# Sixteen expert tiles of a decoder layer run between the last eleven steps of its attention part

## The chip, the core and the metric

One core of one Trainium2 chip runs the whole kernel. The metric is the device time of one execution in microseconds (us), lower is better. The engines are TensorE (PE in the profile; PEld is its weight load), VectorE (DVE), ScalarE (ACT), GpSimd (POOL) and SyncE (SP). Each runs its own queue of instructions strictly in order and waits for the others through semaphores; SyncE and GpSimd also issue the DMAs.

## The reference, cut to what matters

```python
def reference(x, ctx, mask, ...):                       # x: (4, 1024, 256)
    # linear attention, 16 heads of 16
    q, k, v = softmax(x @ Wq.T + bq), softmax_over_tokens(x @ Wk.T + bk), x @ Wv.T + bv
    a = layernorm(q @ (k.T @ v)) * ln_g + ln_b
    x = layernorm(x + a @ Wo.T + bo)
    # cross attention, 8 heads of 32 over 77 context rows, masked
    x = layernorm(x + softmax(x/sqrt(32) @ K.T + b + mask) @ V)
    # mixture of experts: 8 experts, the best 4 of each token
    w, idx = top_k(softmax(x @ router_w), 4);  w = w / w.sum()
    y = sum_j w_j * gelu(x @ up_w[idx_j]) @ down_w[idx_j]     # 256 -> 1024 -> 256
    return layernorm(x + y)
```

The layer norms of the last two lines have neither scale nor shift. All inputs and outputs are float32.

## The kernel before

4096 tokens in four batches are 32 token tiles of 128. The kernel has two parts, one after the other.

**Attention (`attention`).** A software pipeline of 49 steps (`STEPS`) over the token tiles. Each step does one stage for each of up to six tiles: `a` the projections to queries, keys and values, and `c0` to `c4` (`chain_tile(s, d)`) the later stages of older tiles: head outputs and first normalization (`c0`, `out`, tile `Z`), output projection, residual and second normalization (`c1`, `wo`, `X1`), logits against the context (`c2`, `lg`), probabilities turned and multiplied by the context values (`c3`, `pa`, `pb`, `pv`, result `X2`), and the third normalization, the turned tile and the router's logits (`c4`, `x2`, `rt`). Every ninth step has no tile and closes a batch (`closing`). From step 35 on there are no new tiles (`a`), so steps 38 to 48 only drain `c0` to `c4`; step 38 has no `c3`, step 39 no `c4`, step 44 no `c0`, step 45 no `c1`, and so on. The third normalization needs GpSimd twice: `second_residual` adds `X1` to `X2` (line 532), and `inverse_deviation` makes the reciprocal deviation (lines 519 and 521), in the next step. In every step GpSimd does its work in a fixed order: deviations, two record scatters, second residual, residual bias (line 527), two record scatters.

For each half batch VectorE ranks the experts (`choose`, `gates`), and GpSimd scatters one 64-byte record (token, weight) per token and expert into `slot_records` in DRAM (line 548, 128 DMAs in all). `store_tile` writes each finished tile to `token_sums` (float32) and `token_rows` (split in two float16 parts). Beside this the expert weights come in as 16 pieces of 1 MB (`PIECE_STEPS`, the last at step 40) and are split into float16 pairs by ScalarE and VectorE (lines 616 and 707).

After the last step VectorE makes the tile tables (`tile_tables`, lines 843 to 886): which expert a tile belongs to, where its records lie, and three scales.

**Experts (`experts`).** 72 tiles, 63 of 256 slots and 9 of 128. For each, SyncE loads the records (line 1240), GpSimd gathers the token rows (`gather`, line 1273), SyncE turns them with DMA transposes (line 1247), TensorE makes the up products (line 1321, 48 matmuls in four groups, each in one of four PSUM banks), ScalarE the gelu (line 1359), VectorE splits the result into two halves (lines 1396 and 1398), TensorE makes the down products (line 1335, 48 matmuls), ScalarE scales by the gate (line 1367) and GpSimd adds the result to `token_sums` by an indirect DMA (`result`, line 1282). TensorE does the up products of tile t before the down products of tile t - 1. At the end the sums are loaded, normalized and stored. All memory of the attention part is free for the experts, since the parts do not overlap.

## Time and profile before

| | us |
|---|---|
| median of 3 runs (lowest to highest) | 1327.94 (1326.01 to 1328.0) |
| the profiled execution | 1324.53 |
| its span, first to last instruction | 1322.5 |
| TensorE busy | 1124.3 (85%) |
| VectorE busy | 744.9 (56%) |
| GpSimd busy | 660.8 (50%) |
| ScalarE busy | 477.0 (36%) |

The span falls into three parts. Up to 523 us the attention steps run, with all engines in use and none of them full. From 523 to 559 us TensorE does next to nothing: the last records, the tables and the first gather. From 559 to 1280 us the experts run with TensorE always busy. The last 42 us are the final normalization. Times in the rows are microseconds from the start of the span.

### The profile page before, as it was taken

How to read it: one execution, taken by the hardware profiler on the slowest of the kernel's cores; microseconds unless marked ns; L12 is line 12 of the kernel's file. 1: busy time of each engine (PE TensorE's matmuls, PEld its weight loads, DVE VectorE, ACT ScalarE, POOL GpSimd, SP SyncE). 2: the span in 40 equal slices, each digit the busy share in tenths (PEclk: the TensorE clock that was granted, in tenths of full speed). 3: DMA queues.
4: the chain of work that ended last, by engine and by line, in shares of the span. 5: the costliest groups of instructions: out<-in, count | busy, mean ns of one | idle time of the engine just before them, and what ended most of it. 6: DMA issues, size and time to landing. Idle time of an engine off the chain costs nothing.

```text
span 1322.5 us, 26761 instructions
## 1 busy us (share of the span) xinstructions
PE 1124.3 (85%) x8570; PEld 924.5 (70%) x8570; DVE 744.9 (56%) x1803; ACT 477.0 (36%) x896; POOL 660.8 (50%) x769
## 2 busy tenths in 40 slices
PE   5569888888987872099999999999999999999980
PEld 3246665655665652088888888888888888888860
DVE  2667868777887774264444555444555444454325
ACT  3754434434533430033333333333333333333223
POOL 3023437737757776534445555445555444554424
PEclk9779879878977875599999999999999999999995
DMA  6531212222221110145444444444444445443426
GB/s 199 161 109 46 75 34 78 80 64 58 67 69 48 57 36 24 40 65 81 76 79 78 79 78 79 79 78 80 75 78 80 81 75 79 79 78 61 66 38 254
DMA packets 159965, 103.78 MB, mean 78 GB/s; under 512 B 104908, under 2 KB 151168, under 8 KB 159584
## 3 DMA queue, kind: packets, MB, share of 16 engines
q1 hardware_dynamic: 129824, 65.62, 19.4%
q0 software_dynamic: 30016, 36.46, 17.1%
q8 instruction: 83, 1.36, 0.4%
q14 instruction: 42, 0.34, 0.1%
HBM read 50.38 MB, written 33.95 MB: 64 GB/s over the span
## 4 chain that ended last, share of the span: by engine, by line
PE 55%; DMA 1%; DVE 1%; POOL 1%; issue 1%; SPq 0%; ACT 0%; ACTq 0%; POOLq 0%; DVEq 0%
PE psu L1321 28%; PE psy L1335 27%; POOL frstd L1298 1%; DMA token_sums<-y,rec 1%; DVE fstat L1419 1%; DMA sums<-token_sums 0%; DVE sums L1411 0%; DMA xT<-xg 0%; SPq L1239 0%; POOL fvar L1296 0%; SPq L1240 0%; DVE fmv L1422 0%; SPq L1247 0%; ACT sums L1378 0%; ACTq L1156 0%
## 5 line engine op out<-in xcount | busy, mean ns | idle before, releaser
L1321 PE MATMUL psu<-xT,w_up 128*128 128x256 f16 (+1 forms) x3456 | 379.8, 268 | 37.3 <-DMA xT<-xg 37.3
L1282 POOL DMA_INDIRECT token_sums<-y,rec x135 | 223.8, 1658 | 332.5 <-ACT y L1367 308.1
L1321 PEld LDWEIGHTS psu<-xT,w_up 128*128 x3456 | 326.5, 98 | 80.7 <-issue 38.8
L1335 PE MATMUL psy<-w_down,hh 128*128 x2160 | 357.6, 273 | 0.0
L1335 PE MATMUL psy<-w_down,hl 128*128 x1080 | 294.4, 273 | 0.0
L1359 ACT ACTIVATE h<-psu,up_scale 128x512 f32<-128x512 f32 x270 | 185.5, 687 | 179.8 <-PE psu L1321 135.7
L1335 PEld LDWEIGHTS psy<-w_down,hh 128*128 128x128 f16 x2160 | 211.2, 98 | 25.6
L1398 DVE SCALAR_TENSOR_TENSOR hl<-h,h_scale,hh 128x512 f16<-128x512 f32 x270 | 202.9, 752 | 9.6
L1396 DVE TENSOR_SCALAR hh<-h,h_scale 128x512 f16<-128x512 f32 x270 | 132.3, 490 | 91.1 <-ACT h L1359 78.9
L1386 DVE TENSOR_SCALAR gate<-rec,y_scale 128x2 f32<-128x2 f32 (+1 forms) x72 | 16.3, 227 | 292.9 <-ACT y L1367 279.5
L1367 ACT ACTIVATE y<-psy,gate 128x256 f32<-128x256 f32 x135 | 57.1, 470 | 312.0 <-PE psy L1335 312.0
L1273 POOL DMA_INDIRECT xg<-token_rows,rec x135 | 133.7, 990 | 52.6 <-issue 40.2
L548 POOL DMA_INDIRECT slot_records<-recs,posi x128 | 131.2, 1025 | 40.2 <-issue 31.7
L1335 PEld LDWEIGHTS psy<-w_down,hl 128*128 128x128 f16 x1080 | 105.6, 98 | 12.1
L519 POOL TENSOR_SCALAR ve<-mv 128x1 f32<-128x1 f32 x96 | 24.1, 251 | 169.3 <-DVE mv L715 167.5
L1053 PE MATMUL big<-wqkv,xinT 128*128 128x512 f32 x128 | 73.5, 704 | 4.0 <-ACT xinT L597 4.0
L521 POOL TENSOR_TENSOR rstd<-ve,nhalf 128x1 f32<-128x1 f32 x96 | 57.0, 594 | 8.1 <-POOL ve L519 0.2
L1120 PE MATMUL small<-vx,pT 128*128 128x99 f32 (+2 forms) x320 | 48.3, 304 | 9.0 <-ACT pT L604 9.0
L1120 PEld LDWEIGHTS small<-vx,pT 128*128 128x128 f32 (+1 forms) x320 | 43.5, 213 | 15.2 <-ACT pT L604 12.0
L1110 PE MATMUL big<-kbd,x1T 128*128 128x308 f32 x128 | 51.2, 484 | 0.0
L999 PE MATMUL trans<-ident,X 128*128 128x128 f32 x128 | 29.3, 315 | 23.9 <-DVE X L719 19.6
L532 POOL TENSOR_TENSOR X<-X 128x256 f32<-128x256 f32 x32 | 32.5, 1014 | 32.1 <-DVE L L969 17.9
(213 smaller groups left out, 1286.9 us busy)
## 6 DMA issues: line engine op xcount, KB each, us to landing
w_down<-in_L_ffn_up_w_dram SPq DMA_DIRECT2D x8, 1024.0 KB, 5.2
w_down<-in_L_ffn_down_w_dram SPq DMA_DIRECT2D x7, 1024.0 KB, 5.8
XA<-in_x_dram SPq DMA_DIRECT2D x32, 128.0 KB
XRES<-in_x_dram SPq DMA_DIRECT2D x32, 128.0 KB
token_sums<-X SPq DMA_DIRECT2D x32, 128.0 KB
token_rows<-XR SPq DMA_DIRECT2D x32, 128.0 KB, 1.7
sums<-token_sums SPq DMA_DIRECT2D x8, 512.0 KB, 6.6
out_dram<-sums SPq DMA_DIRECT2D x8, 512.0 KB, 2.6
```

Of the source, the lines that this page charges most:

```text
L521: pool.tensor_tensor(rstd[:, kind, at:at + 1], ve[:, kind, at:at + 1], nhalf[:, 0:1], ALU.pow).then_inc(rstd_ready[kind], 1)
L548: pool.indirect_dma_start(slots, bass.IndirectOffsetOnAxis(ap=posi[:, half, e:e + 1], axis=0), recs[:, half, e // TOPK, e % TOPK, :], None ...
L1053: pe.matmul(dst[:, 0:2 * C], xT[:, c, :], wqkv[:, c, C:3 * C], start=(c == 0), stop=(c == CC - 1))
L1120: ins = pe.matmul(dst[:, h0 * (XD + 1):h1 * (XD + 1)], pT[0:n, c, :], vx[0:n, c, 0:h1 - h0, :].rearrange("p h d -> p (h d)"), start=(c == ...
L1273: pool.indirect_dma_start(xg[:, t % 2, j, :], None, rows, bass.IndirectOffsetOnAxis(ap=rec[:, t % RING, j, 0:1], axis=0)).then_inc(xg_load ...
L1282: pool.indirect_dma_start(acc, bass.IndirectOffsetOnAxis(ap=rec[:, t % RING, j, 0:1], axis=0), y[:, t % 2, j, :], None, compute_op=ALU.add ...
L1321: ins = pe.matmul(psu[use % UBANKS][:, i * size(t):(i + 1) * size(t)], w[:, ws, c, m:m + P], xT[:, t % 2, xs * CC + c, 0:size(t)], start=( ...
L1335: ins = pe.matmul(ytile(t)[:, j, :], (hh, hl)[hs][:, t % 2, c, j * P:(j + 1) * P], w[:, ws, c, :], start=(n == 0), stop=(n == 3 * HC - 1))
L1359: act.activation(h[:, use % UBANKS, :], psu[use % UBANKS][:, :], ACT.Gelu_apprx_tanh, scale=k["up_scale"][:, t:t + 1]).then_inc(gelu_ready, 1)
L1367: act.activation(y[:, t % 2, j, :], ytile(t)[:, j, :], ACT.Copy, scale=gate[:, t % 2, j:j + 1]).then_inc(y_ready, 1)
L1396: dve.tensor_scalar(hi, hf, k["h_scale"][:, t:t + 1], None, ALU.mult).then_inc(hh_ready, 1)
L1398: dve.scalar_tensor_tensor(out=lo, in0=hf, scalar=k["h_scale"][:, t:t + 1], in1=hi, op0=ALU.mult, op1=ALU.subtract).then_inc(hl_ready, 1)
```

## The change

The first sixteen of the 63 full expert tiles are made from the tokens of batches 0 and 1 alone, whose records are complete by step 35. Every expert's whole tiles of 256 slots are taken from them (`taken`), so that the number of tiles stays 72.

- **One part.** `attention` and `experts` become one function `layer`. `Q` and `K` are separate tensors; the experts' buffers lie over `K`, `wqkv`, `xinT`, `XA` and `V`, which are free from step 38 on.
- **Early copies.** The tiles of batches 0 and 1 are stored to `early_sums` instead of `token_sums`, and to `early_rows` as well as `token_rows`. At the end of step 35 SyncE copies their records to `early_records` (8 DMAs of 128 KB); scatters of batch 2 wait for it (`records_copied`). The last weight piece comes at step 36 instead of 40 and waits for the last key sums.
- **Early tables.** VectorE makes the sixteen early slots in step 36 (`early_slots`) and experts and scales in step 37 (`factors`, `early_scales`). At the end of step 37 GpSimd gathers tiles 0 and 1.
- **Mixed steps.** Steps 38 to 48 (`MIX0` on) each have one expert tile, cut in four groups. TensorE's up products of group i and down products of group i - 2 (`LAG`) stand between the stages of the attention. All up products of these steps go to one PSUM bank, all down products to another. ScalarE copies the turned tiles first and then does the group's gelu; `exp_logits` moves to the next step. GpSimd gathers tile t + 2 after the first two deviations, and adds the result of tile t - 1 at the end of the step.
- **Behind them.** Tiles 11 to 15 run beside the last sixteen scatters (eight before each of two results) and the late tables, which VectorE does in four pieces behind four groups' halves. After tile 15 the records come from `slot_records`; between tiles 18 and 19 SyncE copies `early_sums` to `token_sums` (16 DMAs of 128 KB), and the result of tile 16 waits for it.
- **Groups throughout.** All 72 tiles run as groups with a lag of two, with 3 PSUM banks for up products instead of 4, 2 gelu buffers instead of 4 and 4 buffers for halves.

```diff
-PIECE_STEPS = [2, 3, 4, 5, 6, 7, 8, 9, 12, 16, 20, 24, 28, 32, 36, 40]
+PIECE_STEPS = [2, 3, 4, 5, 6, 7, 8, 9, 12, 15, 18, 21, 24, 28, 32, 36]
+EARLY = 16
+MIX0 = PIECE_STEPS[-1] + 2
+LAG = 2
+HALF_RING = 4
+H_RING = 2
...
+def up_bank(i):
+    return 0 if i < MIXED_GROUPS else (i - MIXED_GROUPS) % 3
...
+                if s == record_step(EARLY_BATCHES) - 1:
+                    for half in range(HALVES):
+                        sp.wait_ge(scattered[half], 16 * HT * TOPK * EARLY_BATCHES)
+                    for e in range(EXP):
+                        at = slice(e * CAP, e * CAP + EARLY_BATCHES * N)
+                        sp.dma_start(slots1[at, :], slots[at, :]).then_inc(records_copied, 16)
+                if s == MIX0 - 2:
+                    for t in range(4):
+                        records(t)
+                if s >= MIX0 - 1:
+                    turned_rows(s - MIX0 + 1)
...
             def scatter(b, half, at, n):
                 pool.wait_ge(records_ready, HALVES * b + half + 1)
+                if b == EARLY_BATCHES:
+                    pool.wait_ge(records_copied, 16 * EXP)
...
+                if s >= MIX0:
+                    gather(s - MIX0 + 2)
...
+                if s == MIX0 - 1:
+                    gather(0)
+                    gather(1)
+                if s > MIX0:
+                    result(s - MIX0 - 1)
+            for t in range(MIXED, ETILES):
+                if t + 2 < ETILES:
+                    gather(t + 2)
+                if t < MIXED + 2:
+                    scatter(B - 1, HALVES - 1, (t - MIXED) * HT * TOPK // 2, HT * TOPK // 2)
+                result(t - 1)
+            result(ETILES - 1)
...
+            for i in range(MIXED_GROUPS - 1, NGROUPS):
+                t, g = GROUP[i]
+                halves(i)
+                if i == MIXED_GROUPS:
+                    late_blocks()
+                if i == MIXED_GROUPS + 1:
+                    late_experts()
+                if i == MIXED_GROUPS + 2:
+                    late_slots()
+                if i == MIXED_GROUPS + 3:
+                    late_scales()
...
+            for i in range(MIXED_GROUPS, NGROUPS):
+                up_products(i)
+                down_products(i - LAG)
```

TensorE in a mixed step of the changed kernel, in the code's own words (each call is one group or one stage):

```python
up_products(i);  turn("z", c1);  turn("q", c0);  down_products(i - LAG)
turn_second(c4);  turn("x1", c2);  heads_out(c0);  up_products(i + 1)
route(c4);  project(c1);  down_products(i + 1 - LAG);  turn_shares(c3)
up_products(i + 2);  context_logits(c2);  down_products(i + 2 - LAG)
context_values(c3);  up_products(i + 3);  down_products(i + 3 - LAG);  positions(s)
```

VectorE's order in such a step is: moments of `c4`, halves of group i - 1, normalization of `c4`, halves of i, head outputs of `c0` with their sums, row gates, router logits, first sum of `c1`, halves of i + 1, normalizations of `c0` and `c1`, low rows of `c4`, halves of i + 2, logits of `c2`, shares and values of `c3`, routing, sums of `c3`.

How the queues read at the places that the prediction speaks of. GpSimd, one full step before (step 42), from the deviation of `c4` to the last scatter; `X<-X` is the second residual and `XRES<-XRES,cvec` the residual bias:

```order
L519 TENSOR_SCALAR ve<-mv 128x1 [waits mv_ready2]
L521 TENSOR_TENSOR rstd<-ve,nhalf 128x1 [waits ve_ready2]
L519 TENSOR_SCALAR ve<-mv 128x1 [waits mv_ready0]
L521 TENSOR_TENSOR rstd<-ve,nhalf 128x1 [waits ve_ready0]
L519 TENSOR_SCALAR ve<-mv 128x1 [waits mv_ready1]
L521 TENSOR_TENSOR rstd<-ve,nhalf 128x1 [waits ve_ready1]
L548 DMA slot_records<-recs,posi 32768x16 [waits records_ready]
L548 DMA slot_records<-recs,posi 32768x16
L532 TENSOR_TENSOR X<-X 128x256 [waits sm_free,x1_ready]
L527 TENSOR_TENSOR XRES<-XRES,cvec 128x256 [waits xres_loaded0]
L548 DMA slot_records<-recs,posi 32768x16 [waits records_ready]
L548 DMA slot_records<-recs,posi 32768x16
```

GpSimd, the same stretch of the changed kernel, from the second residual of one step to the gather of the next:

```order
L766 TENSOR_TENSOR X<-X 128x256 [waits sm_free,x1_ready]
L761 TENSOR_TENSOR XRES<-XRES,cvec 128x256 [waits xres_loaded0]
L784 DMA slot_records<-recs,posi 32768x16 [waits records_copied,records_ready]
L784 DMA slot_records<-recs,posi 32768x16
L814 DMA early_sums<-y,rec 2048x256 [waits y_added0,y_ready]
L814 DMA early_sums<-y,rec 2048x256
L753 TENSOR_SCALAR ve<-mv 128x1 [waits mv_ready2]
L755 TENSOR_TENSOR rstd<-ve,nhalf 128x1 [waits ve_ready2]
L753 TENSOR_SCALAR ve<-mv 128x1 [waits mv_ready0]
L755 TENSOR_TENSOR rstd<-ve,nhalf 128x1 [waits ve_ready0]
L798 DMA xg<-early_rows,rec 128x256 [waits rec_loaded7,xt_loaded1]
L798 DMA xg<-early_rows,rec 128x256
```

Two result DMAs now stand between a step's scatters and the next step's deviation of `c4`, and two gathers between the deviations of `c0` and `c1`. ScalarE before, in a full step (`pr<-pr` is the exponential of the logits):

```order
L597 ACTIVATE zT<-trans 128x256 [waits tr_ready]
L597 ACTIVATE qT<-trans 128x256 [waits tr_ready]
L597 ACTIVATE x1T<-trans 128x256 [waits tr_ready]
L604 ACTIVATE pT<-trans 128x512 [waits sm_ready,tr_ready]
L604 ACTIVATE pT<-trans 104x128 [waits sm_ready,tr_ready]
L664 ACTIVATE XR<-X 128x256 [waits rows_stored1,x2_ready]
L597 ACTIVATE x2T<-trans 128x256 [waits tr_ready]
L668 ACTIVATE pr<-pr 128x616 [waits big_free]
```

ScalarE in a full mixed step of the changed kernel, up to its second gelu and the results behind it (`h<-big` is a gelu):

```order
L876 ACTIVATE zT<-trans 128x256 [waits tr_ready]
L876 ACTIVATE qT<-trans 128x256 [waits tr_ready]
L919 ACT_TABLE_LOAD
L919 ACTIVATE pr<-pr 128x616 [waits big_free]
L876 ACTIVATE x2T<-trans 128x256 [waits tr_ready]
L876 ACTIVATE x1T<-trans 128x256 [waits tr_ready]
L907 ACT_TABLE_LOAD [waits hl_ready]
L907 ACTIVATE h<-big,up_scale 128x512 [waits up_ready]
L925 ACTIVATE XR<-X 128x256 [waits rows_stored0,x2_ready]
L907 ACTIVATE h<-big,up_scale 128x512 [waits hl_ready,up_ready]
L883 ACTIVATE pT<-trans 128x512 [waits sm_ready,tr_ready]
L883 ACTIVATE pT<-trans 104x128 [waits sm_ready,tr_ready]
```

The first gelu now stands behind the copies of both turned tiles and a table load, and a second load stands before the exponential. TensorE in the changed kernel, at the turn of the second sum (`X`, from `X2` and then `X1`) in a full step:

```order
L1683 MATMUL big<-w_down,hh 128x256 x2
L1683 MATMUL big<-w_down,hl 128x256
L1534 MATMUL trans<-ident,X 128x128 [waits tr_copied,x2_ready]
L1534 MATMUL trans<-ident,X 128x128
L1534 MATMUL trans<-ident,X 128x128 [waits tr_copied,x1_ready]
L1534 MATMUL trans<-ident,X 128x128
L1575 MATMUL small<-state,qT 128x136 [waits sm_free,tr_copied]
L1575 MATMUL small<-state,qT 128x136
L1664 ISA [waits gelu_ready]
L1664 MATMUL big<-xgT,w_up 128x256 x2
```

Before, the turn of the second sum ended a step's products and the router product followed it; now the second up group of the tile stands behind it and waits for the first group's gelu.

## Rows read from the trace of the kernel before

**Rows 1.** Windows: stretch, its length, busy (count) by engine, granted clock, DMA share, GB/s
```profile
core 0: us, PE busy (x) PEld busy (x) DVE busy (x) ACT busy (x) POOL busy (x), PEclk, DMA share, GB/s
415.30:523.20 107.90, 71.05 (x328) 53.06 (x328) 68.88 (x218) 29.46 (x68) 77.24 (x108) 0.71 0.16 46
523.20:559.00 35.80, 0.02 (x1) 0.03 (x2) 13.11 (x37) 1.49 (x2) 20.40 (x20) 0.50 0.13 28
```

**Rows 2.** The chain that ended last, start of the expert part: start, length, what
```profile
554.92 1.31 SPq L1247
...
558.98 13.48 PE psu L1321 x96
572.46 5.24 PE psy L1335 x48
```

**Rows 3.** Timeline of TensorE, steps 37 to 40: start, length, instruction, idle before
```profile
414.24 0.42 PE L999 MATMUL trans<-ident,Z 128*128 128x128 f32 x2
...
419.73 0.30 PE L1111 MATMUL big<-mbf,one 1*128 1x308 bf16 x1
423.37 0.69 PE L999 MATMUL trans<-ident,X 128*128 128x128 f32 x2 [3.34 <-DVE X L719]
...
437.11 0.41 PE L999 MATMUL trans<-ident,X 128*128 128x128 f32 x2 [1.58 <-ACT zT L597]
...
443.80 0.38 PE L999 MATMUL trans<-ident,QK 128*128 128x128 f32 x2
```

**Rows 4.** Instructions grouped by line and shape: count, busy us, mean ns, idle before
```profile
L1398 DVE SCALAR_TENSOR_TENSOR hl<-h,h_scale,hh 128x512 f16<-128x512 f32 x270 | 202.9, 752 | 9.6
L1359 ACT ACTIVATE h<-psu,up_scale 128x512 f32<-128x512 f32 x270 | 185.5, 687 | 179.8 <-PE psu L1321 135.7 <-DVE hl L1398 28.3 <-issue 15.6
...
L1396 DVE TENSOR_SCALAR hh<-h,h_scale 128x512 f16<-128x512 f32 x270 | 132.3, 490 | 91.1 <-ACT h L1359 78.9 <-issue 7.7
...
L950 DVE SCALAR_TENSOR_TENSOR pr<-big,bcol,xmb 128x616 f32<-128x616 f32 x32 | 27.2, 851 | 0.1
...
L938 DVE TENSOR_REDUCE xm<-big 128x8 f32<-128x616 f32 x32 | 25.5, 796 | 9.0 <-PE big L1111 8.7
...
L1352 ACT ACT_TABLE_LOAD x1 | 1.3, 1283 | 29.1 <-PEq L208 29.1
```

**Rows 5.** Timeline of GpSimd, step 37's end and step 38's first deviation
```profile
418.12 0.73 POOL L532 TENSOR_TENSOR X<-X 128x256 f32<-128x256 f32 x1
418.80 0.73 POOL L527 TENSOR_TENSOR XRES<-XRES,cvec 128x256 f32<-128x256 f32 x1
...
420.98 0.96 POOL L548 DMA_INDIRECT slot_records<-recs,posi  x1 [0.30 <-issue]
421.97 0.24 POOL L519 TENSOR_SCALAR ve<-mv 128x1 f32<-128x1 f32 x1
422.30 0.57 POOL L521 TENSOR_TENSOR rstd<-ve,nhalf 128x1 f32<-128x1 f32 x1
```

**Rows 6.** Timelines of GpSimd (first gather, a result) and ScalarE (a tile's results)
```profile
550.84 0.99 POOL L1273 DMA_INDIRECT xg<-token_rows,rec  x1 [6.11 <-DMA rec<-slot_records]
...
641.81 1.62 POOL L1282 DMA_INDIRECT token_sums<-y,rec  x1 [4.26 <-ACT y L1367]
643.74 1.70 POOL L1282 DMA_INDIRECT token_sums<-y,rec  x1 [0.30 <-issue]
...
640.70 0.84 ACT L1367 ACTIVATE y<-psy,gate 128x256 f32<-128x256 f32 x2 [4.63 <-PE psy L1335]
```

**Rows 7.** Instructions grouped by line: the split of a weight piece on VectorE
```profile
L707 DVE SCALAR_TENSOR_TENSOR w_down<-V,wsc,w_down 128x2048 f16<-128x2048 f32 x1 | 2.3, 2335 | 0.0
```

**Rows 8.** DMA issues: count, KB each, median us from issue to landing
```profile
w_down<-in_L_ffn_up_w_dram SPq DMA_DIRECT2D x8, 1024.0 KB, 5.2
```

**Rows 9.** Timeline of VectorE: the first and the last instruction of the tables
```profile
523.06 0.17 DVE L843 TENSOR_SCALAR QK<-QK 128x32 f32<-128x32 f32 x1
...
536.36 0.75 DVE L886 TENSOR_REDUCE y_scale<-QK 128x72 f32<-128x576 f32 x1
```

## What I predict, and why

> **What bounds the kernel now.** I read the windows first, then the timelines around two places, then the groups of instructions by line. The windows [rows 1] show three stretches. From 559 us on, TensorE is busy without a gap at full clock, and the rows of the chain [rows 2] give 5.24 us for each half of a tile: an expert tile is worth 10.48 us of TensorE, and nothing but TensorE work bounds it. Before it lie 35.8 us in which TensorE does nothing (last records, tables, first gather). Before that, attention steps 38 to 48 take 107.9 us with TensorE busy for 71.1 us, at a mean granted clock of 0.71. So the change aims at a real hole: 263.0 us pass from the first TensorE instruction of step 38 (414.24, [rows 3]) to the end of the eleventh tile's work (558.98 + 11 x 10.48 + 3.0 for the slow first 96 products of [rows 2] = 677.3). A full step's attention products fit in 6.7 us at full clock (437.11 to the next step's turn of the queries at 443.80, [rows 3]), and I count 50 us for the eleven. With 115.3 us of tiles that is 165 us, 98 us below what is spent now. The question is how much of the 98 the order of the queues gives back.
>
> **A mixed step, from gelu to gelu.** I follow the loop through the engines from G, the end of the step's first gelu; TensorE may then start the second up group, since all groups of the mixed steps share one bank. One group is 1.31 us up and 1.31 us down (a quarter of 5.24).
> TensorE: up 1.3, router products 0.5; the projection waits until VectorE has done two halves (0.49 + 0.75, [rows 4]) and the head sums, so it starts near 2.1 and ends at 3.0; down 4.3, turned shares 5.0, third up group 6.3. ScalarE has by then to copy the shares and send two results (2 x 0.42, [rows 6]), so the third gelu (0.69) ends at 7.6. VectorE does its halves until 9.0, then maximum 0.80, shift 0.23, subtraction 0.85, reciprocal and values some 0.6 [rows 4]: about 11.6 with the small gaps.
> GpSimd: the second residual waits for these values. It takes 0.73 and behind it stand, in this order, the residual bias (0.73), two scatters (2 x 1.27, [rows 5]), and the two result DMAs of the tile before (2 x 1.66 + 2 x 0.30 = 3.9, [rows 6]), and only then the deviation for the next step (0.24 + 0.57, [rows 5]): 20.7. This is the step that I find decisive. The result DMAs, 3.9 us, are issued in front of the deviation on which everything that follows waits.
> Then VectorE scales the tile (0.41, 21.2), TensorE turns it (0.4, as the turn at 443.80 in [rows 3]) and ScalarE copies it (0.9 with the gaps), the copy of the other turned tile adds 0.3, a table load 1.28 [rows 4], the gelu 0.69: the next G is at **24.5 us**. TensorE's work in that time is 17.1 us; it idles 5 us before the turn and 2.5 us before the second up group.
>
> Without scatters and bias (step 44) the same walk gives 20.6; with eight scatters but fewer chains, steps 45 and 46 give 24.5 and 21.5. Step 47 has no exponentials of logits but the shares in step 48 force two table loads between gelus; with four groups each for 47 and 48, the last one ends 20.0 later. Step 38 has no down products, results or second residual, and its end is set by ScalarE (two copies, load 1.28, exponential 0.72, copy, load 1.28, gelu), which gives 17.0 from its G to that of step 39.
>
> ScalarE's switches themselves: [rows 4] shows 1.28 us for a load with the next activation right behind it (the warming gelu that opens the expert part), after a long idle time. The Trainium skill, "ScalarE: Activation LUTs", section "What ACT_TABLE_LOAD costs", says that a switch also drains the engine for about 1.38 us, 2.66 us in all. The row shows the load alone, and no row has a load right behind other work, so the trace neither confirms nor excludes the drain; by the page the ten gelu loads would add some 14 us (an estimate from its figure), by the row nothing.
>
> **Before the first gelu.** (a) All 16 weight pieces are now done before step 38, one more than now: 2.33 us of VectorE and five small instructions [rows 7] on an engine with little room, 2.5 us. (b) In step 36 GpSimd's scatters wait for the copy of the records, which SyncE issues after the last weight piece (at 396.3, when the sums of keys are done): 1 MB in 5 to 6 us each (w_down lands in 5.2, [rows 8]), so near 407 instead of 402.3, 4.7 us. The sixteen small instructions for the early slots (about 0.3 us apiece: 31 take 14.0 us in [rows 9]) run on VectorE in the same time and are hidden by it; alone they would cost the same. (c) The first gather stands behind step 37's last scatter, which ends at 421.94 [rows 5]. Before, the first gather starts at 550.84, the transposes at 554.92 and the product at 558.98 [rows 6, 2], 8.1 us from end to end; with 0.3 of gap that is 430.4, and TensorE, whose queue has the up group ahead of step 38's turns, stands from 414.24: 16.2 us. (d) Up group, turns, copies, load and gelu on an engine at half clock (2.6 + 1.8 + 3.1): 7.5 us.
> Sum until G of step 38: 30.9 us.
>
> **After the mixed steps.** Two down groups are left over, 2.6 us. VectorE then has the late tables: 14.0 us in before (523.06 to 537.1, [rows 9]), and about as much with more but smaller instructions, cut into four pieces behind the halves of four groups. Four groups last 10.5 us on TensorE; halves (5.0) and tables (14.0) take VectorE 19.0. Of the 8.5 us too much the lag of two groups covers 0.9, since the halves before come late too: **7.6 us** of stall on TensorE. The sixteen last scatters (2 x 10.2 us on GpSimd) delay the gathers of tiles 14 and 15 to within a microsecond of need; the copies of 2 MB of sums hold one result for about 8 us where the next gather has 20. Both I cost at nothing, and name them as a rival.
>
> **Clock.** Where TensorE has waited 3.3 us (419.96 to 423.37, [rows 3]) its next turn takes 0.69 us where two such products take 0.38 at full clock; in the empty stretch before the experts the granted clock is 0.50 [rows 1], the 1.2 GHz level, and at 558.98 the slow start behind it cost 3.0 us [rows 2]. With a 7.5 us hole in every mixed step I expect this in ten of them. At most 3.0 us each, at least nothing; some of the slow time lies beside VectorE and GpSimd, so I take half, 15 us.
>
> **The sum.** 30.9 + 17.0 + 5 x 24.5 (steps 39 to 43) + 20.6 + 24.5 + 21.5 + 20.0 + 2.6 = 259.6 us, plus 15 for the clock: 274.6 against 263.0, 11.6 longer, and 7.6 for the tables: 19.2 us. The other 56 tiles' worth and the final norms stay: the groups are cut finer, but per group of 2.62 us VectorE needs 1.24 and ScalarE 0.69. The profiled execution took 1324.5 us (span 1322.5); with 19.2 it is 1343.7. The median of the runs is 3.4 us above it, so I forecast **1347 us**, 1330 to 1362 for this case (loop within 1 us a step, clock between 8 and 25).
>
> **Rivals.**
> *First, faster.* The results do not sit on the loop: GpSimd's order costs nothing because the values come early enough. Then the limit is TensorE's own 17.1 us plus the wait for z, q, exponential, two copies, two loads and gelu (about 3.5 us), 20.5 per step. Five steps win 4.0 each, steps 45 and 46 win 6.5 together: 26 us; the holes shrink to 3 us and the 15 us of clock go: 1347 - 41 = 1306. It decides if the second residual starts before about 8 us after G rather than at 11.7. For it: GpSimd is busy only some 17 of 24.5 us, and reported times overlap by a tenth each, so serial addition is too dear. Against: the order rows show no instruction that could move. 25%, with all between 1306 and 1325.
> *Second, more scarcity behind the mixed steps.* Scatters, the 2 MB of copies and gathers on one GpSimd queue starve tiles 14 to 20: each scatter burst is 10.2 us where GpSimd has 4 us of room per tile (10.48 less 3.9 for results and 2.6 for gathers), so up to 2 x 6 = 12 us: 1359. 10%.
> *Third, still slower.* The table switches cost double when the engine was working (at most another 1.28 on ten gelu loads, 13 us, as an engine in work may show what the idle one of [rows 4] does not; the mechanism is the one of the page named above) and the slow clock takes its full 3.0 in each step (15 more): 1347 + 28 = 1375. For it: no hole of 3 us in before leaves the clock high. 17%.
> *Fourth,* steps and tiles do not mix and simply add: 107.9 + 115.3 = 223.2 us, 39.8 less than 263.0, of which the start takes 30.9 and the tables 7.6, so 1.3 us are won: 1327. It is the case in which the change does not do what it says; it lies inside the range, 6%.
>
> **Chances.** Forecast and its surroundings above 1331: 42%; first rival 25%; second 10%; third 17%; fourth rival 6%. A measurement of this kernel can tell about 0.2% from no change, here 1325.3 to 1330.6. Faster 0.27 (the first rival and a little of the last), same 0.05, slower 0.68. The range leaves out the extreme halves of the first and third rival: 1308 to 1372.
>
> **What would show it.** Right: GpSimd's result rows directly before the deviation row in steps 40 to 43, VectorE idle on the deviation for several us, steps of 24 to 27 us, a hole on TensorE before the turn of the second sum, granted clock below 0.9 between 440 and 700; first up product near 438; tile 11 near 686. Wrong: steps of 20 us with TensorE released by gelu only, clock above 0.95; or holes on TensorE between tiles 14 and 20; or more than 1.3 us between a ScalarE copy and the gelu behind a load. Wrong too if the first up product comes before 430.

## The result, and the profile after

| | before | after |
|---|---|---|
| median (lowest to highest), us | 1326.97 (1325.80 to 1328.00), 4 runs | **1365.95** (1363.79 to 1367.62), 4 runs |
| after / before | | 1.0294, 95% interval 1.0281 to 1.0307 |
| the profiled execution, its span | 1324.53, 1322.5 | 1363.79, 1361.9 |
| TensorE busy, mean granted clock | 1124.3, 0.906 | 1136.4, 0.898 |

The kernel became 39 us slower. The prediction said slower, 1347 us, in a range of 1308 to 1372: direction and range held, but the sum of +19 us was only half of what came, and the narrower range given for the forecast's own case, 1330 to 1362, did not hold. The windows of the changed kernel answer to [rows 1]:

```profile
core 0: us, PE busy (x) PEld busy (x) DVE busy (x) ACT busy (x) POOL busy (x), PEclk, DMA share, GB/s
436.90:686.00 249.10, 187.87 (x1318) 151.47 (x1319) 116.49 (x290) 85.76 (x147) 125.76 (x136) 0.83 0.26 48
...
692.00:726.00 34.00, 21.53 (x147) 15.04 (x145) 19.62 (x54) 4.62 (x8) 22.19 (x21) 0.78 0.24 40
...
780.00:900.00 120.00, 119.88 (x1099) 107.19 (x1097) 58.56 (x103) 40.33 (x68) 63.91 (x47) 1.00 0.54 92
```

From 780 us on all is as it was: TensorE all but full (119.88 of 120 us), 10.48 us a tile. The time is lost in three places:

| place | before | after | lost | forecast |
|---|---|---|---|---|
| from 414.24 to the first product of the twelfth tile | 674.7 (677.3 less the 2.6 that still belong to the eleventh) | 690.8 | 16.1 | 11.6 |
| from there to the last product | 608.0 | 627.8 | 19.8 | 7.6 |
| behind the last product | 39.5 | 43.0 | 3.5 | 0 |

The first row gives points in time, the others lengths. The last products of TensorE start at 1282.72 before and at 1318.62 after, 35.9 us apart; 19.8 is what is left when 16.1 is taken off.

**Inside a mixed step.** The loop that the prediction called decisive stands in the trace as described. Timelines of GpSimd, VectorE, TensorE and ScalarE from the end of step 40 into step 41 (start, length, instruction, in brackets the idle time before it and what ended it):

```profile
500.74 0.42 DVE L1353 TENSOR_TENSOR X<-small,xr 128x256 f32<-128x256 f32 x1
501.31 0.72 POOL L766 TENSOR_TENSOR X<-X 128x256 f32<-128x256 f32 x1 [2.75 <-DVE X L1353]
...
502.53 0.18 DVE L1057 BATCH_NORM_AGGREGATE mv<-stat 128x2 f32<-128x6 f32 x1
502.87 1.09 POOL L784 DMA_INDIRECT slot_records<-recs,posi  x1
504.27 0.96 POOL L784 DMA_INDIRECT slot_records<-recs,posi  x1 [0.30 <-issue]
505.53 1.63 POOL L814 DMA_INDIRECT early_sums<-y,rec  x1 [0.30 <-issue]
507.46 1.58 POOL L814 DMA_INDIRECT early_sums<-y,rec  x1 [0.30 <-issue]
508.49 0.85 POOL L753 TENSOR_SCALAR ve<-mv 128x1 f32<-128x1 f32 x1
509.43 0.57 POOL L755 TENSOR_TENSOR rstd<-ve,nhalf 128x1 f32<-128x1 f32 x1
510.03 0.41 DVE L1061 TENSOR_SCALAR X<-X,mv,rstd 128x256 f32<-128x256 f32 x1 [6.14 <-POOL rstd L755]
510.50 1.12 PE L1534 MATMUL trans<-ident,X 128*128 128x128 f32 x4 [4.37 <-DVE X L1061]
511.65 0.38 ACT L876 ACTIVATE x1T<-trans 128x256 f32<-128x256 f32 x1
512.06 1.28 ACT L907 ACT_TABLE_LOAD   x1
513.35 0.69 ACT L907 ACTIVATE h<-big,up_scale 128x512 f32<-128x512 f32 x1
514.18 2.74 PE L1664 MATMUL big<-xgT,w_up 128*128 128x256 f16 x12 [1.65 <-ACT h L907]
```

The moments are ready at 502.7; the deviation (L753) that needs them starts at 508.49, behind two scatters and two result transfers. VectorE waits 6.14 us for it and TensorE 4.37 us for VectorE. The up group behind the hole takes 2.74 us instead of 1.48, the length that the same row has at full clock.

**Behind the mixed steps** stands something that the prediction did not have. TensorE and GpSimd of the changed kernel beside tile 11:

```profile
692.95 0.99 POOL L784 DMA_INDIRECT slot_records<-recs,posi  x1 [0.30 <-issue]
...
701.86 0.95 POOL L784 DMA_INDIRECT slot_records<-recs,posi  x1 [0.30 <-issue]
...
697.50 0.38 PE L1664 MATMUL big<-xgT,w_up 128*128 128x256 f16 x2 [0.94 <-issue]
698.94 0.27 PE L1664 MATMUL big<-xgT,w_up 128*128 128x256 f16 x1 [1.06 <-issue]
700.35 0.38 PE L1664 MATMUL big<-xgT,w_up 128*128 128x256 f16 x2 [1.14 <-issue]
701.80 0.59 PE L1664 MATMUL big<-xgT,w_up 128*128 128x256 f16 x2 [1.06 <-issue]
703.91 0.58 PE L1664 MATMUL big<-xgT,w_up 128*128 128x256 f16 x2 [1.52 <-issue]
```

An up group and a down group together usually take TensorE 2.6 us. Here one or two products come every 1.4 us, and the profile knows no engine or transfer that they wait for ("issue"). This goes on while GpSimd issues its eight scatters, one every 1.27 us, and again from 717 to 726 us beside the next eight. Between 697.5 and 706.2 the DMA engines are busy for 2% of the time, so it is not their traffic. VectorE works on meanwhile, one small instruction every 0.2 us from 697.15 to 698.79. What TensorE waits for between 690 and 780 us, in sum (us, times, longest):

```profile
PE big L1664 <- issue: 9.0, 10, 1.5
PE big L1683 <- ACT y L915: 1.8, 1, 1.8
PE big L1683 <- issue: 1.7, 2, 1.0
```

### The profile page after: what moved, and what is told of

It reads as the page before. It is cut to its first block, busy times and chain, and to the rows that moved or that the text cites. A ratio compares the mean times of both kernels' runs of the same rounds, so it can differ in the third digit from the quotient of the medians.

```text
span 1361.9 us, 27063 instructions
## 1 busy us (share of the span) xinstructions
PE 1136.4 (83%) x8572; PEld 926.6 (68%) x8572; DVE 752.8 (55%) x1831; ACT 496.6 (36%) x913; POOL 673.0 (49%) x768
## 4 chain that ended last, share of the span: by engine, by line
PE 65%; DVE 10%; POOL 10%; issue 5%; ACT 4%; DMA 4%; SPq 1%; ACTq 0%; POOLq 0%; DVEq 0%
PE big L1664 26%; PE big L1683 13%; PE trans L1683 11%; POOL slot_records L784 3%; PE big L1706 2%; PE big L1605 2%; POOL rstd L755 2%; PE small L1584 2%; PE trans L1534 2%; POOL early_sums L814 2%; PE small L1752 2%; PE small L1616 1%; ACT L907 1%; PE small L1629 1%; POOL X L766 1%
## 5 line engine op out<-in xcount | busy, mean ns | idle before, releaser
L1664 PE MATMUL big<-xgT,w_up 128*128 128x256 f16 (+1 forms) x3456 | 422.8, 272 | 48.6 <-ACT h L907 21.1
L1664 PEld LDWEIGHTS big<-xgT,w_up 128*128 x3456 | 329.3, 100 | 101.8 <-issue 57.8
L907 ACT ACTIVATE h<-big,up_scale 128x512 f32<-128x512 f32 x270 | 185.5, 687 | 459.1 <-PE big L1664 439.1
L1683 PE MATMUL big<-w_down,hh 128*128 x1264 | 221.0, 277 | 3.7 <-ACT y L915 2.0
L1683 PE MATMUL big<-w_down,hl 128*128 x632 | 174.7, 276 | 0.0
L1683 PE MATMUL trans<-w_down,hh 128*128 x896 | 153.9, 274 | 0.0
L1683 PEld LDWEIGHTS big<-w_down,hh 128*128 128x128 f16 x1264 | 125.0, 100 | 21.8 <-issue 4.2
L753 POOL TENSOR_SCALAR ve<-mv 128x1 f32<-128x1 f32 x96 | 29.0, 303 | 217.3 <-DVE mv L1057 216.0
L1683 PE MATMUL trans<-w_down,hl 128*128 x448 | 122.6, 274 | 0.0
L1683 PEld LDWEIGHTS trans<-w_down,hh 128*128 128x128 f16 x896 | 87.9, 98 | 11.1
L814 POOL DMA_INDIRECT early_sums<-y,rec x32 | 53.1, 1661 | 35.9 <-ACT y L915 28.4
L1683 PEld LDWEIGHTS big<-w_down,hl 128*128 128x128 f16 x632 | 62.7, 99 | 9.4 <-issue 1.6
```

Source lines behind the costliest of these rows:

```text
L814: pool.indirect_dma_start(acc1 if t < EARLY else acc, bass.IndirectOffsetOnAxis(ap=rec[:, t % RING, j, 0:1], axis=0), y[:, t % 2, j, :], N ...
L907: act.activation(h[:, i % H_RING, :], psu[up_bank(i)], ACT.Gelu_apprx_tanh, scale=k["up_scale"][:, t:t + 1]).then_inc(gelu_ready, 1)
L1664: ins = pe.matmul(psu[up_bank(i)][:, j * size(t):(j + 1) * size(t)], w[:, ws, c, m:m + P], xgT[:, t % 2, xs * CC + c, 0:size(t)], start=(n ...
L1683: ins = pe.matmul(ytile(t)[:, j, :], (hh, hl)[hs][:, i % HALF_RING, at:at + P], w[:, ws, c, :], start=(c == 0 and j == 0 and hs == 0 and w ...
```

## The experiments

All are the changed kernel with one or two edits. The kernel before was run beside each; its medians were 1325.4, 1326.8, 1327.1 and 1326.3 us in the four sittings, so differences of medians across sittings are good to about 2 us. "Gain" is against 1365.95.

| kernel | median (lowest to highest) | / before, 95% interval | gain |
|---|---|---|---|
| e1 results behind the deviation | 1337.66 (1336.96 to 1339.42) | 1.0090 (1.0065 to 1.0115) | 28.3 |
| e2 without the last 16 scatters | 1350.33 (1347.41 to 1351.58) | 1.0177 (1.0149 to 1.0205) | 15.6 |
| e3 these scatters in fours | 1355.78 (1349.62 to 1361.53) | 1.0218 (1.0171 to 1.0265) | 10.2 |
| e4 one mixed step | 1318.90 (1317.90 to 1320.85) | 0.9949 (0.9933 to 0.9964) | 47.1 |
| e5 = e1 and e3 | 1329.94 (1329.43 to 1338.99) | 1.0033 (1.0017 to 1.0050) | 36.0 |
| e6 no table switches | 1348.45 (1346.13 to 1350.01) | 1.0160 (1.0141 to 1.0179) | 17.5 |
| e7 = e4, scatters in twos | 1308.02 (1306.38 to 1309.66) | 0.9850 (0.9832 to 0.9869) | 57.9 |
| e8 = e7 with two mixed steps | 1308.47 (1307.83 to 1308.92) | 0.9853 (0.9837 to 0.9869) | 57.5 |
| e9 = e7, early gathers | **1305.64** (1302.67 to 1308.77) | 0.9839 (0.9825 to 0.9852) | 60.3 |
| e10 24 filling products a step | 1358.97 (1358.71 to 1364.89) | 1.0243 (1.0227 to 1.0259) | 7.0 |
| e11 = e1, e2 and e6 | 1302.22 (1299.23 to 1305.54) | 0.9817 (0.9798 to 0.9836) | 63.7 |
| e12 40 filling products a step | 1361.63 (1358.14 to 1362.47) | 1.0263 (1.0247 to 1.0280) | 4.3 |

### e1: the results behind the next deviation

```diff
                 if c4 is not None:
                     inverse_deviation(2, c4)
+                if s > MIX0 + 1:
+                    result(s - MIX0 - 2)
...
-                if s > MIX0:
-                    result(s - MIX0 - 1)
+            if MIXED >= 2:
+                result(MIXED - 2)
             for t in range(MIXED, ETILES):
```

> On GpSimd the adding transfers of an early tile (result, 3.9 us in two instructions) stand behind the next step's second deviation (inverse_deviation(2, c4)) instead of before it; nothing else changes. Theory of the loop: in the step from 498.3 to 514.2 us VectorE's moments are there early and the deviation starts only at 508.49, behind two transfers that end at 509, so each of the ten steps gives back 2.5 to 3.9 us, and the slower clock a part more: 1366 comes down to 1328 to 1341. Rival one (the transfers only move: the deviation of the first norm and the gather now stand behind them): 5 to 12 us gained, 1354 to 1361. Rival two (the step is set by VectorE's and TensorE's own order, GpSimd has slack): within 3 us of 1366.

28.3 us: the theory of the loop. The same place in e1, GpSimd and TensorE:

```profile
502.62 0.96 POOL L784 DMA_INDIRECT slot_records<-recs,posi  x1 [0.30 <-issue]
503.60 0.25 POOL L753 TENSOR_SCALAR ve<-mv 128x1 f32<-128x1 f32 x1
503.94 0.57 POOL L755 TENSOR_TENSOR rstd<-ve,nhalf 128x1 f32<-128x1 f32 x1
504.70 1.80 POOL L814 DMA_INDIRECT early_sums<-y,rec  x1 [0.19 <-issue]
...
505.01 0.66 PE L1536 MATMUL trans<-ident,X 128*128 128x128 f32 x4 [0.52 <-DVE X L1063]
508.45 1.48 PE L1666 MATMUL big<-xgT,w_up 128*128 128x256 f16 x12 [2.31 <-ACT h L909]
```

The deviation now stands behind the scatters alone. TensorE waits 0.52 us instead of 4.37, and both the turn and the up group run at full clock. From the first gelu of step 38 to that of step 47 it is 198.6 us instead of 224.1. The gain is the loop's and, with it, what the shorter hole gives back in clock (0.910 for 0.898 over the span). So an order of two lines on an engine that is half idle was worth 28 us, and the kernel that moves them is still 12 us slower than the one before.

### e2 and e3: the last sixteen scatters

e2 takes the two bursts of eight away (and lowers to fit what SyncE waits for ahead of tile 16), so it leaves out those tokens' records; e3 keeps them, four beside each of four tiles, ahead of the gather of that turn:

```diff
+                if t < MIXED + SPREAD:                      # e3: SPREAD = 4; e2: these lines are left out
+                    scatter(B - 1, HALVES - 1, (t - MIXED) * HT * TOPK // SPREAD, HT * TOPK // SPREAD)
                 if t + 2 < ETILES:
                     gather(t + 2)
-                if t < MIXED + 2:
-                    scatter(B - 1, HALVES - 1, (t - MIXED) * HT * TOPK // 2, HT * TOPK // 2)
```

> The last sixteen record scatters (the second half of the last batch), which stand in two bursts of eight beside tiles 11 and 12, are left out, so those tokens' records are missing and part of the output is not the reference's; the tables on VectorE stay. Theory of the scatters (TensorE gets its products about 1.4 us apart just while GpSimd issues a scatter every 1.27 us): TensorE works through 697 to 726 us without the pauses, and 19.6 us lost behind tile 11 come down to 5 to 9: 1366 falls to 1352 to 1356. Rival (the late tables on VectorE hold back the halves and so everything): 0 to 3 us gained, 1363 to 1366.

> The same sixteen scatters, four beside each of tiles 11 to 14 instead of eight beside tiles 11 and 12, put before the gather of the same turn. Theory of the scatters, price by the piece (each holds TensorE up by its 1.27 us whatever stands around it, about 0.8 us lost): nothing changes, 1363 to 1369. Theory of the burst (only a long row of them drains what TensorE has ready): 5 to 10 us gained, 1356 to 1361. Rival (the tables alone cost the time): within 3 us, and TensorE's pauses stay at 697 to 726 us while the scatters are elsewhere.

The same 34 us in e2 and e3 (columns as above; 21.53 us of TensorE work and clock 0.78 in the changed kernel):

```profile
692.00:726.00 34.00, 29.02 (x247) 24.41 (x245) 25.81 (x68) 8.46 (x14) 12.87 (x11) 0.95 0.38 67
...
692.00:726.00 34.00, 27.98 (x195) 19.84 (x194) 22.81 (x57) 7.20 (x13) 20.00 (x18) 0.80 0.29 47
```

Without the scatters 247 products are recorded instead of 147, and no wait of the kind "issue" is left in that stretch. What it does wait for there is the tables' doing:

```profile
PE big L1681 <- DVE hl L1302: 2.5, 3, 1.5
PE trans L1681 <- DVE hl L1302: 2.5, 1, 2.5
```

Those 5.0 us are a wait for VectorE, behind the late tables. The gain of e2 is not all TensorE's. In the profiled executions its first product of the twelfth tile comes 2.1 us later (692.91 for 690.80, a difference that is there before the first scatter is left out), from there to the last product it takes 615.8 us instead of 627.8, 12.1 less, and from the start of that last product to the end of the span 39.7 instead of 43.3, 3.6 less. So the scatters keep TensorE waiting for about 12 us, and of the 19.8 us lost in this stretch 7.7 remain for the tables, where 7.6 had been forecast.

e3 gains 10 of e2's 15.6 us with all scatters still there. Its four runs lie 12 us apart (by its interval the gain is 5 to 18 us), but all lie below the 1363 to 1369 that a price by the piece would give. So the price isn't one by the piece: it hangs on how long GpSimd issues transfers without a break. (e3 and e7 also put the scatters ahead of the gather; no run has the one change without the other.) In e3 GpSimd's transfers (scatters, gathers, results) follow each other unbroken from 692.5 to 711.5 us, and the pauses of TensorE lie between 698 and 713; beside its next row, eight transfers from 720.2 us on, there are two short ones, and beside six transfers from 734.5 to 743.1 us none.

### e4: one mixed step instead of eleven

```diff
-MIX0 = PIECE_STEPS[-1] + 2          # 38
+MIX0 = 48
...
+TABLES0 = PIECE_STEPS[-1]
...
-                if s == MIX0 - 2:                   # early_slots(); early_scales() one step later
+                if s == TABLES0:
```

> MIX0 is 48 instead of 38, with the early tables still built in steps 36 and 37: ten steps run as plain attention steps, one early tile runs in step 48, and 15 run behind the attention beside the last records and tables. Theory (mixing costs more than it hides; the gain of the early tables is only the hole of 35.8 us at the end of the attention): ten plain steps at about 10.2 us each and ten tiles at 10.5 us against 249 us for the mixed stretch save 40 to 50 us: 1316 to 1326, faster than the kernel before by 2 to 12 us. Rival one (the first gather, which waits for records and rows, leaves the same start hole of 16 us at step 48): 1330 to 1340. Rival two (the mixed steps are as good as separate ones and the loss is elsewhere): 1355 to 1366.

47.1 us, and faster than the kernel before by 6. Ten attention steps without tiles and ten tiles without attention are quicker than the ten mixed: from 414 to 530 us the steps run as plain attention steps, then come tiles of 10.48 us. The late scatters and tables together cost what they did: from the first gelu of the second tile to that of the third (545.79 to 575.57) it is 29.8 us where 10.48 are due, 19.3 too many, with the same pauses (7.0 us of "issue") beside one row of 20 transfers.

### e5: e1 and e3 together

> e1_result_later and e3_scatters_in_fours together, eleven mixed steps as in the changed kernel. Theory (two separate losses, 28 us in the mixed steps and about 10 behind them): they add up, 1326 to 1331, level with the kernel before. Rival (with the early tiles done sooner the same wait returns at the late records or sums): 1334 to 1338.

1329.94 us: they add up nearly (28.3 + 10.2 = 38.5, measured 36.0). Two of the ten runs took 1338 and 1339 us; the profile is of one of them, so I read no places from it.

### e6: no table switches

```diff
-                act.activation(h[:, i % H_RING, :], psu[up_bank(i)], ACT.Gelu_apprx_tanh, scale=...
+                act.activation(h[:, i % H_RING, :], psu[up_bank(i)], ACT.Gelu_apprx_tanh if i >= MIXED_GROUPS else ACT.Copy, scale=...
```

> The gelus of the eleven mixed steps' groups are plain copies of the same shape with the same scale, so ScalarE loads no table between them and the exponentials; the values of the early tiles are wrong. Everything else as in the changed kernel. The prediction counted 1.28 us on the path for the gelu table of each step: with one load on the path in ten steps 13 us go, 1350 to 1356. Rival one (a switch also drains the engine, 2.66 us in all): 27 us or more, 1334 to 1341. Rival two (both loads of a step are on the path): about 24 us, 1338 to 1344. Rival three (the load hides in ScalarE's wait): 0 to 4 us.

17.5 us, between the theory's 13 and rival one's 27; the copies leave the early tiles' values wrong. From step 38's first gelu to step 47's it is 208.3 us instead of 224.1, 1.76 per step. The table of instructions by line shows what went, in the changed kernel:

```profile
L907 ACT ACT_TABLE_LOAD x10 | 12.8, 1283 | 0.2
L919 ACT ACT_TABLE_LOAD x8 | 10.3, 1283 | 0.1
```

If the ten loads before the gelus, 12.8 us, are all on the path, as the timeline above has it, the eight before the exponentials (10.3 us) cost the other 3 to 5. The timeline above shows the load at 512.06, 0.03 us behind the end of the copy at 511.65 + 0.38, and the gelu 0.01 us behind the load. The Trainium skill, "ScalarE: Activation LUTs", section "What ACT_TABLE_LOAD costs", adds a drain of about 1.38 us to the load. No row here has room for it, and 1.76 us per step for two switches is well under its 2.66 for one.

### e7 to e9: towards a kernel that gains

e7 takes e4 and e3's lines with `SPREAD = 8`; e8 has `MIX0 = 47` and e1's order besides; e9 is e7 with

```diff
-                if s == MIX0 - 2:
+                if s == TABLES0 + 2:               # SyncE: records(0) to records(3) in step 38
...
+                if s == TABLES0 + 4:
+                    turned_rows(0)
...
-                if s == MIX0 - 1:
+                if s == TABLES0 + 4:               # GpSimd: in step 40
                     gather(0)
                     gather(1)
```

> e4_one_mixed_step with its sixteen last scatters two at a time beside tiles 1 to 8, before the gather of the same turn. In e4 the tiles behind the first lose about 19 us while GpSimd issues eighteen transfers in 28 us without a break. Theory of the burst (TensorE runs out of products only behind some 6 us of unbroken transfers on GpSimd): two scatters, two gathers and two results take 9 of 10.5 us with a break in between, so 12 to 16 us are gained: 1303 to 1307. Rival (a price by the piece, or the tables on VectorE): 1315 to 1320.

> As e7, but with MIX0 at 47: steps 47 and 48, which hold only the last pieces of the attention, each take a tile, with the adding transfers behind the second deviation. In the changed kernel step 47 with its tile takes 14.0 us and 48 11.6, while a tile alone takes 10.5 and a plain step about 10. Theory (a step without the first norms has room for a tile): 2 to 6 us below e7. Rival (the records for the last batch then come later and the late tables wait for VectorE): as e7 or up to 5 us above it.

> As e7_one_mixed_in_twos, but the records of the first four early tiles are loaded in step 38 and the rows of tiles 0 and 1 gathered and turned in step 40, eight steps before they are used; in e7 TensorE waits 7.15 us for the turned rows of tile 0 at 530.2 and then runs at half clock. Theory: this wait goes, and some of the slow clock behind it: 4 to 10 us below e7, 1298 to 1304. Rival (the last attention step, whose turn waits 9.65 us for VectorE, takes the time instead): 1306 to 1310.

e7 is 10.9 us below e4, a little less than the 12 to 16 I had expected. With two scatters a tile TensorE's waits of the kind "issue" sum to 0.5 us. The 34 us behind the attention in e4, and in e7:

```profile
549.00:583.00 34.00, 21.88 (x136) 14.78 (x134) 18.86 (x49) 5.81 (x10) 21.07 (x20) 0.75 0.17 29
...
549.00:583.00 34.00, 28.98 (x259) 24.70 (x258) 25.19 (x61) 9.65 (x17) 20.92 (x18) 1.00 0.37 62
```

GpSimd is busy for the same 21 us in both, with 20 and 18 instructions, and only TensorE's count differs, 136 against 259. This is the cleanest pair: the same sixteen scatters begin at the same place and are spaced otherwise, and the time behind the last product is the same in both. e8 is e7 over again (1308.47): a second mixed step neither gains nor loses. e9 is 2.4 us better than e7, less than the 4 to 10 expected. TensorE's wait for the turned rows (7.15 us in e7) is gone, and the up group follows the last attention step at once, at 528.06. But that step's turn of the second sum comes 5.0 us later (the first line is e7's, the second e9's):

```profile
520.85 0.69 PE L1537 MATMUL trans<-ident,X 128*128 128x128 f32 x2 [9.65 <-DVE X L1064]
...
525.81 0.69 PE L1540 MATMUL trans<-ident,X 128*128 128x128 f32 x2 [9.64 <-DVE X L1067]
```

Most of the 5 us are lost in one place. GpSimd's second residual starts 0.7 us later than in e7 in step 40 (455.87 for 455.15) and 5.0 us later in step 41 (470.21 for 465.18). In between e9 issues its four gathers, from 460.00 to 464.77 us, in front of the deviation for the next step, which starts at 464.80; in e7 it starts at 459.00, right behind the scatters. It is e1's lesson once more: transfers ahead of the small instruction on which the next stage waits. The up groups of this tile run at half clock in both (2.74 us, three times).

The intervals of e7 and e9 touch (the two were run in different sittings, which alone can move a difference by about 2 us), so e9's own gain is likely rather than shown. Against the kernel before it is 21.4 us, 1.6%.

### e10 and e12: what the clock costs

```diff
                 if i >= LAG:
                     down_products(i - LAG)
+                if i >= LAG and c4 is not None:
+                    idle = turn_into(("x2", c4))[:, :, :].rearrange("p a b -> p (a b)")[:, CC * P:CC * P + FILL_COLUMNS]   # 192
+                    for _ in range(FILL):           # 24 in e10, 40 in e12
+                        pe.matmul(idle, k["wu"][:, 0, 0, 0, 0:P], k["wu"][:, 0, 0, 0, 0:FILL_COLUMNS], start=True, stop=True, skip_group_check=True)
                 if c4 is not None:
                     turn_second(c4)
```

> The changed kernel with 24 products of 128x128 by 192 columns, which nobody reads, in nine of the ten mixed steps just before TensorE waits for the second sum to turn; 2.0 us at full clock, in a hole of 4.4 to 6.8 us. Theory of the clock (the prediction's 15 us: the hole lowers the clock and the work behind it is slow): the granted clock of the mixed steps rises from 0.83 to 0.90 or more and 6 to 15 us go, 1351 to 1360. Rival one (the slow work lies beside what VectorE and GpSimd do): the clock rises, but the time stays within 3 us of 1366. Rival two (the fill delays the turn, or the hole that is left still lowers the clock): 1366 to 1385 with a clock as before.

> As e10_fill_the_hole with 40 products instead of 24, 3.6 us at full clock in the holes of 4.4 to 6.8 us. e10 left one span unchanged (1363.0, its turns at full clock, the up group behind them still at 2.74 us) and three runs 7 us shorter. Theory of the clock: with the hole all but closed the granted clock of the mixed steps passes 0.90, the up group takes 1.5 us, and the time falls below e10's, 1345 to 1356. Rival (the slow clock is mostly not on the path that sets the step): the clock rises and the time is that of e10 or the changed kernel's, 1357 to 1368.

The mixed steps (443 to 668 us) in the changed kernel, in e10 and in e12:

```profile
443.00:668.00 225.00, 165.63 (x1160) 133.41 (x1160) 105.72 (x263) 75.04 (x130) 119.70 (x132) 0.83 0.24 46
...
443.00:668.00 225.00, 181.29 (x1357) 148.84 (x1355) 105.56 (x262) 75.77 (x130) 117.81 (x130) 0.86 0.23 45
...
443.00:668.00 225.00, 186.90 (x1507) 156.59 (x1505) 106.53 (x266) 77.50 (x135) 120.58 (x132) 0.91 0.23 47
```

The granted clock rises from 0.83 to 0.91, TensorE's wait for the second sum falls from 38.7 to 13.8 us in sum, and the time falls by 4.3 us (e10: 7.0, though its profiled execution had steps of the old length). That is less than the 6 to 15 that the clock theory expected for e10, and far less than its 10 to 21 for e12. In the profiled execution of e12 the nine steps from the first gelu of step 38 to that of step 47 are 217.8 us for 224.1, 6.4 less, but its first gelu comes 3.4 us later (447.48 for 444.09), before any filling product. The code up to there is the same, and the first up product comes at 436.9 us in the changed kernel, 438.8 in e2 and 440.4 in e12: single executions differ by that much. Where e12 got an up group to full clock, the first half of its step went as the prediction's walk says; VectorE's values stand at 553.03 + 0.42, 11.8 us behind the end of the step's first gelu (541.69), and the forecast was 11.6:

```profile
541.83 1.48 PE L1665 MATMUL big<-xgT,w_up 128*128 128x256 f16 x12 [2.15 <-ACT h L908]
...
553.03 0.42 DVE L1354 TENSOR_TENSOR X<-small,xr 128x256 f32<-128x256 f32 x1
```

In the same step of the changed kernel, where the up group takes 2.74 us, the stretch is 12.5 us (540.68 to 553.13), 0.7 more:

```profile
552.71 0.42 DVE L1353 TENSOR_TENSOR X<-small,xr 128x256 f32<-128x256 f32 x1
```

In steps 41, 44 and 45 it is 13.8, 13.8 and 12.8 us in the changed kernel and 12.4, 12.3 and 11.6 in e12. e12 closes the hole only in part: in step 41 its up group still takes 2.74 us. So 4 to 7 us is what these fillings gave back, a lower bound of what the clock costs; 0.7 to 1.5 us is what the first halves of these single steps won. That the clock costs the full 15 us is not shown.

### e11: all three causes out

> Eleven mixed steps, with the three suspected costs out at once: results behind the deviation (as e1), no last sixteen scatters (as e2, records missing), plain copies in place of the mixed steps' gelus (as e6, values wrong). Theory (three separate costs of 28, 16 and 17 us): 1303 to 1309. Rival (they overlap: with one gone another fills its wait): 1318 to 1330.

1302.22 us, the sum of the single gains (28.3 + 15.6 + 17.5 = 61.4; measured 63.7). The three costs add up. A mixed step now takes 19 us (461.46 to 480.63, 499.58, 518.53 and 537.49 for its first gelus), and the granted clock is 1.00 from 461.5 to 537.5 us and 0.95 from 443 to 622 us without a product added.

## Why the prediction was right in sign and too small

1. **Start, (a) to (d): right.** First up product forecast near 438, seen at 436.9; end of step 38's first gelu 445.1 forecast, 444.1 seen. TensorE's wait for the first turned rows is 15.6 us, forecast 16.2.
2. **The results on the loop: right.** It was the step called decisive, and e1 gives it its price: 28 us for moving 3.9 us of issue in ten steps, less than 3.9 each because the deviation then stands behind the scatters. The first rival (results not on the loop, 1306) fell.
3. **The steps one by one: nearly right.** Forecast without the clock 17.0, 5 x 24.5, 20.6, 24.5, 21.5, 20.0 (the last two steps, up to the twelfth tile's first product) = 226.1, and with 15 us of clock 241.1; seen 19.5, 129.0 for the five, 24.1, 27.2, 24.4, 22.6 = 246.7 (from unrounded times). In the full steps 41 to 43 the second half, from VectorE's values to the next first gelu, takes 12.9, 12.9 and 13.1 us, where 24.5 - 11.6 = 12.9 was forecast. The terms of the walk as written add to 24.8, not 24.5 (21.2 + 0.4 + 0.9 + 0.3 + 1.28 + 0.69), so the loop over GpSimd is sized to some 0.3 us, and the closer agreement is a slip that happened to help. The first half takes 13.8, 12.5 and 13.4 us for 11.6. Too small were steps 44 to 46: 75.7 us for 66.6, of which 4.5 are what I counted for the clock. In step 44 I took the scatters and the bias off, and not what the step has besides, the ranking of a half batch on VectorE (`routing`), ahead of the statistics of the next tile. The end of that step in the changed kernel:

```profile
608.64 0.19 DVE L1154 TENSOR_TENSOR posx<-small,ebase 128x32 f32<-128x32 f32 x1 [2.00 <-PE small L1639]
...
610.51 0.29 DVE L1173 TENSOR_REDUCE recs<-eqp 128x16 f32<-128x128 f32 x1
...
611.44 0.38 POOL L753 TENSOR_SCALAR ve<-mv 128x1 f32<-128x1 f32 x1 [0.52 <-DVE mv L1057]
611.90 1.06 POOL L755 TENSOR_TENSOR rstd<-ve,nhalf 128x1 f32<-128x1 f32 x1
```

The deviation waits 0.52 us for the statistics behind the results, and takes 0.38 + 1.06 us where I had 0.24 + 0.57: 1.2 us, and 2.2 more in the slow first half, make the 3.5 by which this step is longer than forecast.

4. **The clock: the mechanism right, the size not settled.** 15 us for ten steps are 1.5 each; steps 39 to 43 are 6.5 us over the walk, 1.3 each, all of it in the half that begins with a slow up group. That this half is longer for the clock alone is argued, not shown. Taking part of the slow clock away gave 4 to 7 us (e10, e12).
5. **The table switches: right.** One load of 1.28 per step was counted, with no drain; e6 measures 1.76 for both of a step. The third rival's doubling of the switches fell.
6. **Behind the mixed steps: this is the step that failed.** I wrote: "The sixteen last scatters (2 x 10.2 us on GpSimd) delay the gathers of tiles 14 and 15 to within a microsecond of need ... Both I cost at nothing". The gathers were indeed in time. But beside the scatters TensorE's products come late, for about 12 of the 15.6 us that e2 gains, and spacing them gives most of it back: 10.2 us with fours (e3), 10.9 with twos (e7 against e4, with 0.5 us of such waits left). The second rival had the right place and the right price (up to 12 us), but another mechanism, starved gathers, and I gave it 10%. The tables, forecast at 7.6 us of stall, leave 7.7 where the scatters are gone, 5.0 of them in waits for VectorE.
7. **The tail: 3.5 us that I did not have.** From the last of ScalarE's normalizations to the end of the span it is 3.1 us in the kernel before and 6.2 in the changed one. The last output packet ends 2.3 us behind that normalization in both. What comes later is GpSimd: its closing drain, an instruction that the traces hold and the timelines leave out, starts at the same place and takes 4.6 us before and 7.9 after. The span is 3.1 us in e2, e4, e7, e8, e9 and e11 too (drains of 1.4 to 3.8 us), and 5.6 to 6.2 in e1, e3, e5, e6, e10 and e12 (7.3 to 7.9 us). What the first group has in common is one or two mixed steps, or eleven without the late scatters. Why the drain is longer is open.
8. **The fourth rival** (steps and tiles only add) is what e4 built, in a better way: there the mixed loop's cost is gone and the hole's filling stays.

In short, of the 20.2 us by which the sum was short, 12.2 lie behind the mixed steps, in a cost that I had named and set at nothing; 4.5 up to the twelfth tile, most of it in steps 44 to 46; and 3.5 in the tail, in GpSimd's drain. That 1366 still fell inside 1308 to 1372 is in part luck: the upper end had been widened for the third rival, whose doubled table switches the runs do not show.

## What to carry to other kernels

Work that is slipped between the stages of a latency-bound loop must not issue its transfers ahead of the small instruction on which the next stage waits: on a half idle engine such an order cost 28 us, and putting it right took two lines. Interleave only where a step has room; one mixed step and the rest in the hole, with the scatters in twos, beat the kernel before by 1.5 to 1.6%, eleven mixed steps lost 2.9%. And spread GpSimd's indirect transfers: sixteen of them in two bursts cost TensorE 10 to 12 us here, two per tile next to nothing.

## What the runs showed of the hardware that I had not expected

- **Beside a long row of indirect transfers on GpSimd TensorE's products come late.** I followed GpSimd's unbroken rows (next transfer within 0.6 us) in five kernels behind the attention. Rows of 12 to 20 transfers, 16 to 27 us long, all bring pauses of some 1 us between TensorE's products, from 6 to 17 us after the row's start to at most 2 us after its end (changed kernel: 686.4 to 702.8 and 706.4 to 723.6 us, pauses at 697.5 to 703.9 and 718.2 to 725.3). A row of 8 (e3, 11.6 us) brings two of 0.26 and 0.46 us, those of 6 (in e1, e3 and e7, 8 to 9 us) one of 0.28 and one of 0.16 among nine rows, and a looser row of 10 in e7 none. DMA engines are 2 to 3% busy in the pauses of the changed kernel. Waits of the kind "issue" sum to 10.7 us in the changed kernel between 690 and 780 us, 7.0 in e4, none in e2, 0.5 in e7. What is shared is not settled. A reason that suggests itself is that TensorE's own program comes late: the profile lists queues that carry instructions among the DMA queues. The traces speak against it. Queue 8 brings 83 packets of 16 KB, one for every 256 or so instructions of TensorE. In the changed kernel they start at 693.1, 713.8 and 734.4 us and take 1.0 to 1.4 us, and TensorE leaves its pauses at 704 and 725 us with no packet on its way. The queues from 693 to 706 us, where the one packet of queue 8 is that of 693.1, and from 706 to 712 (queue, kind, packets, MB, share):

```profile
q0 software_dynamic: 312, 0.20, 6.6%
q1 hardware_dynamic: 315, 0.07, 2.6%
q8 instruction: 1, 0.02, 0.7%
...
q0 software_dynamic: 252, 0.24, 36.2%
q14 instruction: 1, 0.01, 0.4%
```

In e1, e3 and e4 too no packet of queue 8 starts during the pauses. But each series of pauses there and in the changed kernel begins 4 to 7 us behind the start of such a packet, so that a link with the supply of instructions isn't excluded.

- **The load of a table right behind work took its 1.28 us and nothing more** (512.06 to 513.35, between a copy and a gelu).
- **The granted clock is not settled by one hole.** Behind holes of 4.37 and 1.65 us the up group takes 2.74 us (the 1.2 GHz level) in the changed kernel; behind 0.52 and 2.31 us it takes 1.48 (2.4 GHz) in e1. In e12, behind 1.07 and 2.15 us in both cases, it takes 2.74 us at 516.98 and 1.48 at 541.83, so what decides at that size stays open.
